# A state-space mixer kernel on one core: small TensorE work regrouped into three PSUM banks, the convolution summed in place, a seventh state buffer, and two of the four state planes added by DMA

## The reference

```
h      = x W^T + b + 2 * (x A_s^T) B_s            # adapter s chosen per sequence
u,gate = split(h W_in^T)                          # 2048 channels each
u      = silu(causal_conv4(u) + conv_b)
dt,B,C = rmsnorm of the parts of u Wx^T           # 64, 16 and 16 rows
delta  = softplus(dt Wdt^T + dt_bias)
state  = exp(delta*A) * state + (delta*u)*B       # 16 states per channel, scanned over 256 tokens
y      = sum over 16 states of (state*C) + u*D
x      = x + (y * silu(gate)) W_out^T
x      = x + experts(cond2(x))                    # top-2 of 8 low-rank experts, softmax weights
```

## Time and profile before

| | |
|---|---|
| median of 3 runs | 2611.05 us (2610.78 to 2613.91) |
| the profiled execution | 2611.66 us, of which the span of its instructions 2609.9 us |
| mean granted TensorE clock | 0.95 |
| busy, us | PE 2321.2, DVE 2239.9, POOL 2121.8, ACT 1622.4 |
| the gating `y_gate` of chunk 0, 16, 32, 112, 127 starts at | 175.3, 548.4, 842.0, 2291.3, 2556.4 us |

### The profile page before, as it was taken

The page is one execution under the profiler, slowest core; times in us unless marked ns, Lnnn a source line. Parts: engine busy times, 40 slices in busy tenths (PEclk is TensorE's granted clock), DMA queues, the critical chain, the costliest instruction groups (busy, mean ns, idle before and its releaser), DMA issues.

```text
span 2609.9 us, 30425 instructions
## 1 busy us (share of the span) xinstructions
PE 2321.2 (89%) x10128; PEld 1911.7 (73%) x10128; DVE 2239.9 (86%) x2084; ACT 1622.4 (62%) x3751; POOL 2121.8 (81%) x1092
## 2 busy tenths in 40 slices
PE   8977998799989999899989999899988987786968
PEld 6866675488777878688777878688777866665857
DVE  1277777589999999999999999999999999999892
ACT  1466555466667766776667766776667766775550
POOL 0087776689889998999889998999889998999770
PEclk9988998899999999899999999899999999888989
DMA  6352433434346434543336434544336333522322
GB/s 213 125 199 85 113 105 111 129 124 137 113 127 199 140 128 131 182 145 137 113 127 199 141 128 131 182 145 137 112 107 202 126 108 101 170 92 97 121 84 97
DMA packets 131511, 350.04 MB, mean 134 GB/s; under 512 B 38609, under 2 KB 43217, under 8 KB 129883
## 3 DMA queue, kind: packets, MB, share of 16 engines
q1 hardware_dynamic: 108600, 296.18, 35.1%
q10 hardware_dynamic: 22756, 51.92, 6.0%
...
## 4 chain that ended last, share of the span: by engine, by line
PE 55%; POOL 14%; DVE 13%; ACT 9%; issue 7%; DMA 1%; ACTq 0%; SPq 0%; POOLq 0%; DVEq 0%
PE ubank L573 9%; PE gbank L594 8%; PE late L639 8%; DVE scan L1196 7%; POOL st L1396 6%; POOL st L1404 6%; ACT scan L1038 4%; PE gbank L603 4%; PE small L555 3%; PE late L674 3%; DVE st L1208 3%; PE late L555 3%; PE scan L573 2%; PE small L755 2%; PE late L613 2%
## 5 line engine op out<-in xcount | busy, mean ns | idle before, releaser
L1196 DVE TENSOR_TENSOR_SCAN scan<-scan,st 128x1024 f32<-128x1024 f32 x512 | 1153.4, 2285 | 192.5 <-ACT scan L1038 171.8
L1396 POOL TENSOR_TENSOR st<-w_sb,bc 128x1024 f32<-128x1024 f32 x512 | 1196.9, 2358 | 77.7 <-PE gbank L603 49.8
L1038 ACT ACTIVATE scan<-delta,A_sb 128x255 f32<-128x255 f32 x2048 | 846.5, 459 | 0.0
L1404 POOL TENSOR_TENSOR st<-st 128x1024 f32<-128x1024 f32 x256 | 603.0, 2356 | 214.9 <-DVE st L1208 204.9
L594 PE MATMUL gbank<-h,wt 128*128 128x256 f32 x2048 | 488.3, 394 | 20.1 <-DVE yg L1222 19.4
L594 PEld LDWEIGHTS gbank<-h,wt 128*128 128x128 f32 x2048 | 402.7, 198 | 93.2 <-DVE yg L1222 27.1
L1208 DVE TENSOR_TENSOR st<-scan,bc 128x1024 f32<-128x1024 f32 x384 | 455.2, 1213 | 0.0
L573 PE MATMUL ubank<-h,wt 128*128 128x256 f32 x1712 | 419.2, 401 | 0.0
L639 PE MATMUL late<-yg,wt 128*128 128x256 f32 x1792 | 401.2, 382 | 0.0
L1035 ACT ACTIVATE scan<-iota 128x4 f32<-128x4 f32 x512 | 86.6, 169 | 501.3 <-DVE st L1208 455.9
L573 PEld LDWEIGHTS ubank<-h,wt 128*128 128x128 f32 x1712 | 348.1, 204 | 58.2 <-issue 3.6
...
## 6 DMA issues: line engine op xcount, KB each, us to landing
wt<-in_W_in SPq DMA_DIRECT2D x256, 512.0 KB, 3.7
wt<-in_W_out SPq DMA_DIRECT2D x128, 512.0 KB, 3.3
wt<-in_cond_W SPq DMA_DIRECT2D x64, 512.0 KB, 3.6
bc<-bc_rows ACTq DMA_DIRECT2D x64, 512.0 KB, 6.5
wt<-G_tiles SPq DMA_DIRECT2D x32, 512.0 KB, 3.7
wt<-in_ffn_B SPq DMA_DIRECT2D x32, 512.0 KB, 3.4
xb<-in_x SPq DMA_DIRECT2D x8, 1024.0 KB, 6.2
...
```

The costliest lines, as they stand in the source:

```text
L1038: last = fn(t[:, k, 1:T], delta[:, c, 1:T], ACT.Exp, scale=A_sb[:, col:col + 1])
L1196: v_.tensor_tensor_scan(Tps[q % 2][:, :], Tps[q % 2][:, :], x_, 0.0, ALU.mult, ALU.add).then_inc(scan_done, 1)
L1396: tt(st[:, n % ST_RING, :, :], w_sb[:, i % 2:i % 2 + 1, :].to_broadcast([P, NQ, T]), bc[:, 0, q * NQ:(q + 1) * NQ, :], ALU.mult).then_inc( ...
L1404: tt(st[:, n % ST_RING, :, :], st[:, n % ST_RING, :, :], st[:, (n - 1) % ST_RING, :, :], ALU.add).then_inc(add_done, 1)
```

## The change

**Banks.** The jobs are dealt to three places, `late`, `small` and the upper half of `gbank` (`half_job`), in an order that differs: PE's slot is now late job, small job, `sum_states(i-1)`, half job, then (after a wait, `ubank_free`) the u projection, the gate projection, and the `xp` or `dt` job of two slots per block. The gate projection goes to the upper half of `ubank`. `cond` chunks 6 and 7, which were one job, are two, `wout` comes one slot later, and one `B` job is cut in two (`Bs`). The small `g` products against the gate's matrix are part of the large ones (264 + 248 columns, in two banks), the bias row is worked on in four column groups and stored by eight DMAs, where there were two. `sel` and `GTg` are no longer loaded.

**Convolution.** The sum starts and stays in the half of PSUM in which the projection was. ACT's `u_evac` waits for its own copy in between, and runs one slot later than before; so do the taps, and they stand elsewhere in DVE's order.

**Planes.** `add_first` is gone and quarter 1's product goes to `st` as the others do. Two accumulating DMAs on POOL's queue (`add_dma`) add plane 0 to plane 1 and plane 1 to plane 2; each moves 512 KB within SBUF and reads what it adds to. POOL still adds plane 3 and folds. The ring has seven planes.

**Softmax.** The eleven short DVE instructions of the routing stand between the scans of slot 11, not in one piece at the end of slot 9.

```diff
-ST_RING = 6
+ST_RING = 7
...
-                return small[:, :]
-            return ubank[:, :]
+            return late if NC <= v < NC + 10 and v % 2 else ubank
+
+        def cv_home(v):
+            return quarter(v % 4)[:, T:2 * T] if v < NC else u_home(v)[:, 0:T]
 
...
+            def ubank_free(i):
+
+                pe.wait_ge(q_done, i + 1)
+                if i:
+                    for v in u_chunks(i - 1):
+                        pe.wait_ge(u_done, v + 1)
+                    if part_job(i - 1):
+                        part, k = part_job(i - 1)
+                        pe.wait_ge(part_ev, PAIRS * part + k + 1)
...
                 for k in range(KH):
-                    last = mm(gbank[:, 0:T], wt[:, n % W_RING, k, :], h0[:, b % 3, k, :],
+                    last = mm(ubank[:, T:2 * T], wt[:, n % W_RING, k, :], h0[:, b % 3, k, :],
                               start=(k == 0), stop=(k == KH - 1))
                 last.then_inc(gate_mm, 1)
 
             def sum_states(i):
-                pe.wait_ge(add_done, 3 * i + 3)
-                pe.wait_ge(q_done, min(i + 2, CHUNKS))
+                pe.wait_ge(add_done, 2 * i + 2)
+                if i:
...
+                else:
+                    pe.wait_ge(pc_ev, 2 * KH)
+                if takes_half(i):
+                    pe.wait_ge(*emptied(takes_half(i)))
+                if part_job(i):
+                    part, k = part_job(i)
+                    pe.wait_ge(part_ev, PAIRS * part + k + 1)
                 n = 4 * i + 3
                 for k in range(2):
                     last = mm(gbank[:, 0:T], ident[:, :], st[:, n % ST_RING, k, :], start=(k == 0), stop=(k == 1))
...
             for i in range(CHUNKS):
                 us = u_chunks(i)
+                if late_job(i):
+                    run(late_job(i), i)
+                if small_job(i):
+                    run(small_job(i), i)
                 if i:
                     sum_states(i - 1)
-                if first_job(i):
-                    run(first_job(i), i)
+                if half_job(i):
+                    run(half_job(i), i)
                 if i == 0:
                     for m in range(4, KH):
                         pro_cond(1, m)
-                if us:
-                    if us[0] % NC == 0:
-                        h0_ready(us[0] // NC)
-                    pe.wait_ge(u_done, us[0])
-                    u_chunk(us[0])
-                if part_job(i):
-                    out_part(*part_job(i))
-                if late_job(i):
-                    run(late_job(i), i)
-                if len(us) > 1:
-                    if first_job(i):
-                        pe.wait_ge(*emptied(first_job(i)))
-                    u_chunk(us[1])
-                if last_job(i):
-                    run(last_job(i), i)
+                ubank_free(i)
+                for v in us:
+                    if v % NC == 0:
+                        h0_ready(v // NC)
+                    u_chunk(v)
...
-                    act.wait_ge(u_done, v)
-                fn(up[:, e, TAPS - 1:], o[:, 0:T], ACT.Copy)
-                fn(o[:, T:2 * T], o[:, 0:T], ACT.Identity, bias=cb[:, c:c + 1],
+                fn(up[:, e, TAPS - 1:], o[:, 0:T], ACT.Copy).then_inc(up_ev, 1)
+                if v >= NC:
+                    act.wait_ge(up_ev, v + 1)
...
-                act.wait_ge(gate_mm, i + 1)
-                if i >= 2:
-                    act.wait_ge(yg_done, i - 1)
-                fn(qg[:, i % 2, :], gbank[:, 0:T], ACT.Silu).then_inc(q_done, 1)
-                fn_exp_table()
-                if job and job[0] == "ms":
-                    evac(job)
                 decay(i, 2)
                 if c == 15 and b < LAST:
                     load_C(b + 1, 0)
+                act.wait_ge(gate_mm, i + 1)
+                if i:
+                    for v in u_chunks(i - 1):
+                        u_evac(v)
+                    if half_job(i - 1) and half_job(i - 1)[0] != "Bs":
+                        act.wait_ge(yg_done, i - 1)
+                        evac(half_job(i - 1), i)
+                if c == 13 and b < LAST:
+                    ms_evac(small_job(i))
                 decay(i, 3)
                 if c == 15 and b < LAST:
                     load_C(b + 1, 1)
                     load_B(b + 1, 3)
-                if job and job[0] in ("dt", "wT"):
-                    evac(job)
-                for v in us:
-                    u_evac(v)
+                if i >= 2:
+                    act.wait_ge(yg_done, i - 1)
+                if i and part_job(i - 1):
+                    part, k = part_job(i - 1)
+                    act.wait_ge(part_ev, PAIRS * part + k + 1)
+                if i:
+                    for v in u_chunks(i - 1):
+                        act.wait_ge(conv_step, 3 * v + 3)
+                fn(qg[:, i % 2, :], ubank[:, T:2 * T], ACT.Silu).then_inc(q_done, 1)
+                if i:
+                    for v in u_chunks(i - 1):
+                        u_silu(v)
+                fn_exp_table()
                 if i == 0:
                     for m in range(4, KH):
                         pro_cond(1, m)
                 if c == 13 and b < LAST:
                     store_rows(b + 1)
...
+                if i:
+                    for v in u_chunks(i - 1):
+                        for k in range(TAPS - 1):
+                            conv_tap(v, k)
+                if weigh:
+                    soft_max_step(b - 1, 5)
                 scan(i, 2)
                 if c == 13 and b < LAST:
                     norm(b + 1)
                 scan(i, 3)
-                if i:
-                    y_sum(i - 1)
-                if first_job(i) and first_job(i)[0] == "wb":
-                    evac(first_job(i))
+                mul(i, 2)
+                if b and c == 10:
+                    soft_max_in(b - 1)
+                mul(i, 3)
                 if i:
                     if i == NC - 1:
-                        dve.wait_ge(G_st, 16 * (KH - 1))
+                        dve.wait_ge(G_st, 16 * KH)
                     if i == NC + 1:
                         dve.wait_ge(*made(("bias", 0, 0)))
+                    y_sum(i - 1)
                     y_gate(i - 1)
-                mul(i, 2)
-                mul(i, 3)
-                for v in u_chunks(i):
-                    for k in range(TAPS - 1):
-                        conv_tap(v, k)
-                if b and c == 9:
-                    soft_max_out(b - 1)
-
-            between(CHUNKS)
...
-                if q == 2 and i:
-                    pool.wait_ge(mul_done, 4 * i - 2)
-                if q == 1 and i >= 2:
+                if q == 2 and i >= 2:
                     pool.wait_ge(id_mm, i - 1)
+                if q == 3 and i:
+                    pool.wait_ge(acc_st[0], 16 * i)
                 tt(st[:, n % ST_RING, :, :], w_sb[:, i % 2:i % 2 + 1, :].to_broadcast([P, NQ, T]),
                    bc[:, 0, q * NQ:(q + 1) * NQ, :], ALU.mult).then_inc(dbu_done, 1)
 
+            def add_dma(i, k):
+                n = 4 * i + k
+                pool.wait_ge(mul_done, n + 1)
+                if k == 2:
+                    pool.wait_ge(acc_st[0], 16 * (i + 1))
+                pool.dma_start(st[:, n % ST_RING, :, :], st[:, (n - 1) % ST_RING, :, :], accum_op=ALU.add
+                               ).then_inc(acc_st[k - 1], 16)
+
             def add(i, k):
                 n = 4 * i + k
-                if k == 3:
-                    pool.wait_ge(add_done, 3 * i + 1)
+                pool.wait_ge(acc_st[1], 16 * (i + 1))
                 pool.wait_ge(mul_done, n + 1)
                 tt(st[:, n % ST_RING, :, :], st[:, n % ST_RING, :, :], st[:, (n - 1) % ST_RING, :, :], ALU.add
                    ).then_inc(add_done, 1)
...
                 for b, j in softplus_of(i - 1):
                     delta_add(b, j)
-                if i + 1 < CHUNKS:
+                if not last:
                     weight(i + 1)
                     for q in range(3):
                         dbu(i + 1, q)
-                add(i, 2)
+                add_dma(i, 2)
+                if not last:
+                    dbu(i + 1, 3)
                 add(i, 3)
                 fold(i)
-                if i + 1 < CHUNKS:
-                    dbu(i + 1, 3)
 
 
```

548 lines of the change are left out of this document (288 added, 260 removed).

## The result

| | before | after |
|---|---|---|
| median, us | 2611.66 (2610.78 to 2613.91) | 2693.83 (2687.39 to 2700.84) |
| profiled span, us | 2609.9 | 2685.6 |
| mean granted TensorE clock | 0.950 | 0.925 |

Each median is that of four runs. The ratio is 1.0314 (1.0279 to 1.0348). The forecast was 2570 with a range of 2515 to 2725: the time is inside the range, but the change made the kernel slower where it was forecast to make it faster. Rival A came true, with 82 us lost where it was priced at 113.

A forecast was written before the change was run, and what follows sets the result against it. DVE was taken to bound the middle blocks, POOL nearly level; 2611.66 - 73 (block 0) + 20 (blocks 1 to 5) + 13 (block 6) - 1 (block 7) = 2571, median 2570 us; range 2515 to 2725.

The forecast's parts named there:

- Rival A: POOL's addition of plane 3 waits for the second DMA; slower, 2725 us at X 4.85, decides from X 3.8; chance 0.35.
- tap wait: DVE stands before the convolution taps for ACT's `u_evac`, 1.8 us in each slot that has a u chunk.
- I: POOL's time to issue one accumulating DMA, two a slot; taken as 0.9 us, between 0.44 and 1.3.
- block 0: First 16 slots: bank waits go, 373.1 us becomes 300, a gain of 73.
- L: Second DMA's time from issue to landing, less the issue; taken as 4.0 us, ends 3.0 and 5.8.
- X: What DMA additions put on POOL's slot, 2 I + (L - 2.35): 3.45 us, ends 1.35 and 6.05.
- blocks 1 to 5: 80 slots, 1464.5 us before: DVE 1474, POOL 1453, 10 added for imperfect overlap, 1484; a loss of 20.
- Block 6: POOL's 16 slots of 17.85 us plus 5 give 291 us against 278.4, a loss of 13.
- Block 7: Up to its last `y_gate`, POOL bounds it without convolution: 264 us against 265.1, a gain of 1.
- DVE's 1474: DVE's time in blocks 1 to 5: less 102 for work, plus 144 for tap wait, waits -43 + 10.
- B: DMA additions cheap, X under 3, tap wait stands, DVE alone bounds; 2537 us; chance 0.17.
- C: No tap wait either: DVE 15.9 us a slot, POOL 15.8, some 2360 us in all; chance 0.04.

The follow-up runs named there:

- e1: The changed kernel with both DMA additions undone, DVE and POOL adding the planes again; 2556.80 us, 0.9793 of before.
- e2: The changed kernel with only the first of the two DMA additions, POOL adding planes 2 and 3 itself; 2564.79 us, 0.9816 of before.
- e9: The changed kernel with most weight tiles from the 40th on loaded to one eighth (64 KB); 2577.90 us, 0.9866 of before.
- e11: e1 with the taps behind the third scan and the `xp` job ahead of the projections; 2559.02 us, 0.9788 of before.
- e12: e2 with the taps behind the third scan and the `xp` job ahead of the projections; 2563.82 us, 0.9812 of before.
- e5: The changed kernel with each DMA addition at half its size (256 KB), the other halves left out of the sum; 2558.24 us, 0.9798 of before.
- e3: The changed kernel with the three taps moved from ahead of the third scan to behind it; 2693.41 us, 1.0322 of before.

## Why the prediction was wrong

**What was right.** DVE's clean slot (17.7 forecast, 17.6 measured) with its tap wait (1.8, 1.57), which gives back what `add_first` took (e1 against e2); the issue, I = 0.9 (it takes 0.873 us, the next instruction starts 0.61 us after it begins and is some 0.3 us longer: `dbu` 2.64 behind an issue, 2.33 apart from one); the first DMA hidden by 8 us of cover (8 us in all, e2); and the place of the gain, block 0, though it was 51 us and not 73.

**The step that failed: L,** the time from the second DMA's issue to its landing. "Less the issue, the ends are 3.0 and 5.8; I take 4.0, nearer the first, whose writes are the same." With the issue that is 4.9 from issue to landing; the page has 5.5 as the median, and POOL's slot on the mean 0.61 + 2.65 + 2.76 = 6.0. The wait is a mean, and landings go from 4.3 to 11.2 us, so a median understates it. In the prediction's terms L was 5.1. (The lower ends were also worked out wrongly: as 6.2 less an issue of 0.44 is 5.8, 3.7 less 0.44 is 3.3 and not 3.0, and an L of 3.0 gives X = 2 x 0.44 + 0.65 = 1.5 and not 1.35.) X became 4.6 and not 3.45, above the 3.8 from which the text says that rival A decides. POOL's slot in blocks 1 to 5 then is 14.4 + 1.8 + 2.9 of waiting for the DMA (228.8 us in the 80 slots of that stretch), and 0.5 for POOL's other waits, which the sum had at nothing but the borders: 19.6. It measured 1561.9 / 80 = 19.5, where the forecast had 17.85 for POOL and 1484 / 80 = 18.55 for the slot. Before it was 18.3, and 1.2 x 80 is the loss of these blocks.

**Why L was too small.** One cause is shown: traffic was priced only at the borders, and e9 shows 0.9 us of the median landing from the weight stream. What the rest comes from stays open: with that stream light a landing is still 4.6 us, where a load of 512 KB from SP took 3.7. That the addition reads what it adds to may be it, but no run separates the reading from the issue on POOL. The DMA engines' share went from 0.44 to 0.70: the new transfers are themselves nearly all of that, 26.6% of the engines' time in the software queue. A resource that was 0.44 busy was priced as if it were to stay so.

By the fit of the Trainium skill's page "DMA: Bandwidth & Descriptors" (section Anatomy of one DMA) a DMA issued from GpSimd would take an estimated 3.2 us for 512 KB and 2.6 for 256 KB. This isn't borne out here: 5.5 us for 512 KB, 4.6 with light traffic, 3.9 for half the bytes. The same page of the Trainium skill says that DMAs from different engines interleave on the same 16 engines (section Issuing engines are not separate DMA queues). The trace agrees: the weight loads went from 3.7 to 4.4 us.

**Block by block.** Block 0: 321.9 against 300 forecast. e1 has 318.7 with DVE's own work back, so 19 of the 22 us are not the DMAs' but the sum's own: it took DVE for the bound of the block, and what bounds it there was not taken apart. Blocks 1 to 5, forecast 1484: the 78 us above it come with L: 1.1 us more in each of 80 slots is 88. Block 6: 301.6 against 291, L again. Block 7: POOL's waits make +6 of -1.

**Right by luck: DVE's 1474.** The prediction reads that DVE bounds the middle blocks and PE only single slots, and its sum for DVE with the tap wait, 1474, is near e1's 1468.2. But e11 and e12 have DVE's clean slot 0.4 and 0.9 us shorter and take 1466.2 and 1461.8. Its terms, 42 us more for the clean slot and 33 less for the waits, happen to add up to a time that DVE's own slot doesn't set. The miss doesn't come from this, since POOL bounded these blocks.

**The rivals.** A was right in place and price: 2725 at X = 4.85, less 112 x 0.29 for X = 4.56, is 2693, and 2694 was measured. That the sum agrees to 1 us is luck, since its blocks are off and cancel: block 0 took 321.9 us against A's 313, and block 6 took 301.6 against 311 (316 less 16 x 0.29); block 7 is some 10 too high as well. Its threshold of 3.8 is consistent too: at 3.6 e9 is still 34 us under before. B's condition, X under 3, is all but met in e5 with 3.1: 2558 us and not 2537, of which block 0 is 17 (317.3 against 300). C didn't come: the tap wait is there, 1.57 us, and behind the third scan it returns as the scan's own (e3).

The chances were off in one place: 4.0 for a bound between 3.0 and 5.8 left X 0.35 below the threshold. The middle, 4.4, gives X = 3.85, at the threshold, and even odds.
